# A spilled operand fetched as 32 by 32 blocks and turned by VectorE, in five of eight groups of a four-layer graph network

## The chip, the cores and the metric

The kernel runs on one core of one Trainium2 chip, in one launch. The metric is the device time of the launch in microseconds, the median of several runs. The profile's engine names are used: PE is TensorE, DVE is VectorE, ACT is ScalarE, POOL is GpSimd, SP is SyncE, which here only issues DMAs.

## The reference

The input `x` has 16 batches of 512 nodes with 128 channels; `adj` is a 512 by 512 matrix. Four layers follow one another, and each is added to its input and layer-normalised over the channels:

```python
x = _layernorm(x + _L0_gnn_ref(x, adj, ...), axis=-1)
x = _layernorm(x + _L1_gnn_ref(x, adj, ...), axis=-1)
x = _layernorm(x + _L2_gnn_ref(x, adj, ...), axis=-1)
x = _layernorm(x + _L3_gnn_ref(x, adj, ...), axis=-1)
```

The change concerns the end of the second one. Its batch normalisation needs sums over all batches, so its outputs are first written out and scaled later:

```python
x = agg.reshape(-1, d)
h = jax.nn.relu(_batchnorm(x @ W1.T + b1, g1, be1))
out = h @ W2.T + b2
out = _batchnorm(out, g2, be2)
```

The third layer is two graph convolutions and then LSTM cells over windows of 1, 2, 3 and 4 nodes. The fourth is eight Euler steps with `adj`, computed as powers of a matrix.

## The kernel before

`first_half` computes the first two layers for all batches. It leaves the second layer's outputs, before their batch normalisation, in DRAM as `o2_spill` (printed `o_spill`), one image of 128 channels (partitions) by 512 nodes for each batch, and the first layer's results as `x1_spill`. `second_half` computes the rest in 8 groups of `GB = 2` batches, `g = 0` to 7; `n = 2g + j` counts batches.

A group passes through a pipeline of steps. In step `g` the LSTM cells of group `g` run (eleven of them, `c = 0` to 10: cells 0 and 1 are window length 1, one for each batch; 2 and 3 are length 2; 4 to 6 length 3; 7 to 10 length 4), and between the cells stand pieces of other work: the fourth layer of group `g - 1`, its last part and the output of group `g - 2`, and the front of group `g + 1`. Which piece stands behind which cell is written out by hand in lists, one table for each engine: `FILL_PE`, `FILL_ACT`, `FILL_DVE`, `FILL_POOL`, `FILL_SP`. List 0 stands behind cell 0, list 1 behind cell 1, and so on to list 10, which stands behind the last cell. Steps 2 to 6 use the `FILL` tables and carry the fronts of groups 3 to 7; step 1 uses `NEXT`, step 0 `ONCE`, the start `START`. Every engine works through its own list in order and waits on semaphores.

The front of a batch runs so before the change:

- SP `prep` (L1339, L1342) loads `o2` (printed `xt`) and the first layer's `x2` (printed `x`); for `j = 0` this is `ahead_0` in list 4 of the step before, for `j = 1` `prep_1` in list 0.
- ACT `prep` (L1506) applies the batch normalisation, one ACTIVATE over 128 by 512, with `scale2` and `shift2` as one value per channel, that is per partition. `ahead_0` stands in list 10 of the step before, `prep_1` in list 4.
- PE `turn` (L1908) transposes the four 128 by 128 tiles into a PSUM bank: `turn_0` in list 1, `turn_1` in list 5.
- DVE `turn` adds that bank to `x2` (L1666) and takes the layer normalisation's statistics in four instructions (L1644), in the same lists.
- POOL `turn` (`root`, L1390 to L1399) makes scale and shift of them in ten small instructions.
- ACT `norm` (L1496 four times, L1515) applies them, in list 2 and in list 6; POOL `norm` (L1416) makes the low part, SP `norm` stores the result, and PE `gather0` (list 3 and list 8) multiplies it by `adj`.

Three waits of PE matter around it. Cell 2 begins on PE with

```python
pe.wait_ge(state_ready, CELLS * g + first)
```

with `first = 2`, so it waits for DVE's last instruction of cell 1 (L1638, the low half of the state). A later cell of the same window waits for `st_l` (L1629) before its last four matmuls (L1896). And `power1a_0` (list 2, for the fourth layer) waits for `x3_lo`, which POOL's `x3split_0` (L1425) sets. Products of two split operands are three matmuls, L141 to L143.

Of the kernel before, what the change touches and what calls it, by code (L numbers as in the profile page):

```python
# [54 lines left out]
def program(nc, x_t, adj_n, adj_t, nv1_t, nv2, l0_w, l0_b, w1_t, bn1, w2_t, bn2, wg, bg0, bg1,  # L55
            wih_t, whh_t, bih, bhh, alpha, l3_w_t, l3_d, fc_w, fc_b, eye, out):
    o2_dram = nc.dram_tensor("o2_spill", (B, P, N), F32, kind="Internal").ap()
    x1_dram = nc.dram_tensor("x1_spill", (B, P, N), F32, kind="Internal").ap()
    x2_dram = nc.dram_tensor("x2_spill", (B, P, N), F32, kind="Internal").ap()
    with ExitStack() as whole:  # L60
        def sem(name):
            return whole.enter_context(nc.semaphore(name))
# [29 lines left out]
        second_half(nc, sem, psum, wg_parts, banks, ident, exponent, scale2, shift2, adj_h, adj_l, wih_h, wih_l, whh_h, whh_l,  # L92
                    wg_h, wg_l, gate_bias, row_sums, x1_dram, o2_dram, x2_dram, raw, xt, x1, small, steps, out)

# [877 lines left out]
def second_half(nc, sem, psum, wg_parts, banks, ident, exponent, scale2, shift2, adj_h, adj_l, wih_h, wih_l, whh_h, whh_l,  # L972
# [8 lines left out]
    with ExitStack() as ctx:  # L981
# [215 lines left out]
        def outputs(c, source, ones, twos):  # L1197
# [255 lines left out]
        def _(act):  # L1453
# [45 lines left out]
            def prep(g, j):  # L1499

                n = GB * g + j
                if not at_start(n):
                    act.wait_ge(front_loaded[j], 32 * g)
                elif n == 0:
                    return
                nc.scalar.activation(o2[j], o2[j], ACT.Identity, scale=scale2[:, 0:1], bias=shift2[:, 0:1]).then_inc(normed2, 1)  # L1506
# [361 lines left out]
        def _(pe):  # L1868
# [231 lines left out]
            def bias():  # L2100
                pe.wait_ge(vt_kept, 1)
                pe.wait_ge(bc_kept, 1)
                for t in range(NT):
# [65 lines left out]
```

## Time and profile before

| | us |
|---|---|
| runs of the kernel before, median of 3 | 919.82 (918.21 to 920.14) |
| the profiled execution, its own time | 921.33 |
| its span in the trace | 919.5 |
| one step (steps 2 to 6 repeat within 0.05) | 83.77 |
| PE busy in the span | 885.8 |
| DVE busy | 664.0 |
| ACT busy | 564.0 |
| POOL busy | 339.1 |

The profiled execution lies 1.51 above the median, and 1.8 of it lies outside the span. An instruction's duration includes its latency, and neighbours on one engine overlap by some tenths; what an instruction costs in a stream is the distance from its start to the next one's. The idle time that the profile prints for PE is time between modelled ends, so short waits show only in those distances. The step from 623.20 to 706.97 (step 4) is read as the example of all five.

### The profile page before, as it was taken

How to read it: one execution, taken by the hardware profiler on the slowest of the kernel's cores; microseconds unless marked ns; L12 is line 12 of the kernel's file. 1: busy time of each engine (PE TensorE's matmuls, PEld its weight loads, DVE VectorE, ACT ScalarE, POOL GpSimd, SP SyncE). 2: the span in 40 equal slices, each digit the busy share in tenths (PEclk: the TensorE clock that was granted, in tenths of full speed). 3: DMA queues.
4: the chain of work that ended last, by engine and by line, in shares of the span. 5: the costliest groups of instructions: out<-in, count | busy, mean ns of one | idle time of the engine just before them, and what ended most of it. 6: DMA issues, size and time to landing. Idle time of an engine off the chain costs nothing.

```text
span 919.5 us, 14510 instructions
## 1 busy us (share of the span) xinstructions
PE 885.8 (96%) x4966; PEld 768.8 (84%) x4966; DVE 664.0 (72%) x1583; ACT 564.0 (61%) x1233; POOL 339.1 (37%) x550
## 2 busy tenths in 40 slices
PE   8999999988989999999999999999999999999996
PEld 6888985466877799888989998898989899978986
DVE  5988886886687766667677667767676777665744
ACT  5676766935755674677377547745763775466341
POOL 3777875621023520342153136214421631340221
PEclk9999999999999899999999999999999999999999
DMA  5412201320110101012001201010120001001000
GB/s 188 148 60 71 74 29 69 138 70 1 35 59 1 35 12 47 1 47 65 5 13 35 70 1 36 24 58 1 47 69 1 12 12 47 1 11 36 1 24 23
DMA packets 26594, 38.54 MB, mean 42 GB/s; under 512 B 3333, under 2 KB 12422, under 8 KB 26010
## 3 DMA queue, kind: packets, MB, share of 16 engines
q1 hardware_dynamic: 26088, 36.05, 11.7%
q10 hardware_dynamic: 434, 1.57, 0.5%
q8 instruction: 39, 0.64, 0.3%
q14 instruction: 33, 0.27, 0.1%
HBM read 21.89 MB, written 15.73 MB: 41 GB/s over the span
## 4 chain that ended last, share of the span: by engine, by line
PE 47%; DVE 12%; ACT 8%; POOL 7%; issue 5%; ACTq 0%; DVEq 0%; POOLq 0%
PE psum L141 14%; PE psum L143 13%; PE psum L142 13%; PE psum L1892 2%; PE psum L1893 2%; ACT gate L1465 2%; PE psum L1896 2%; POOL out_rstd L1398 1%; DVE x_stats L1644 1%; DVE x L1666 1%; DVE in_h L1634 1%; POOL node_l L1416 1%; POOL x_rstd L1398 1%; ACT raw L1496 1%; ACT gate L1468 1%
## 5 line engine op out<-in xcount | busy, mean ns | idle before, releaser
L1465 ACT ACTIVATE gate<-psum,gate_bias 128x256 f32<-128x256 f32 (+2 forms) x296 | 143.4, 556 | 62.0 <-PE psum L1896 53.0
L141 PE MATMUL psum<-in_h,wih_h 128*128 128x256 f32 (+2 forms) x312 | 106.8, 342 | 7.3 <-DVE in_l L1638 5.0
L143 PE MATMUL psum<-in_h,wih_l 128*128 128x256 f32 (+2 forms) x312 | 103.5, 332 | 0.0
L142 PE MATMUL psum<-in_l,wih_h 128*128 128x256 f32 (+2 forms) x312 | 102.8, 329 | 0.0
L1432 POOL TENSOR_TENSOR gate<-in_h,in_l 128x512 f32<-128x512 f32 x14 | 17.9, 1307 | 157.5 <-DVE in_l L1638 157.5
L141 PEld LDWEIGHTS psum<-in_h,wih_h 128*128 128x128 f32 x312 | 58.8, 188 | 19.2 <-DVE in_l L1638 9.1
L1468 ACT ACTIVATE gate<-cell 128x512 f32<-128x512 f32 (+2 forms) x80 | 40.3, 503 | 51.2 <-DVE cell L1622 39.7
L1619 DVE TENSOR_TENSOR gate<-gate 128x256 f32<-128x256 f32 (+2 forms) x48 | 24.0, 501 | 61.3 <-ACT gate L1465 61.2
L142 PEld LDWEIGHTS psum<-in_l,wih_h 128*128 128x128 f32 x312 | 59.0, 189 | 5.5 <-issue 0.5
L143 PEld LDWEIGHTS psum<-in_h,wih_l 128*128 128x128 f32 x312 | 58.8, 189 | 4.6
L141 PE MATMUL psum<-e_h,shared 128*128 128x384 f32 x180 | 61.4, 341 | 0.2
L143 PE MATMUL psum<-e_h,shared 128*128 128x384 f32 x180 | 60.6, 336 | 0.0
L142 PE MATMUL psum<-e_l,shared 128*128 128x384 f32 x180 | 60.6, 336 | 0.0
L141 PE MATMUL psum<-shared 128*128 128x512 f32 x140 | 56.9, 407 | 1.3 <-DVE shared L1744 0.7
L1892 PE MATMUL psum<-st_h,whh_h 128*128 128x256 f32 (+2 forms) x192 | 56.7, 313 | 1.2 <-DVE st_h L1627 1.2
L1425 POOL TENSOR_TENSOR shared<-raw,shared 128x512 fp32r<-128x512 f32 x14 | 18.2, 1303 | 104.8 <-ACT shared L1535 104.8
L1893 PE MATMUL psum<-st_h,whh_l 128*128 128x256 f32 (+2 forms) x192 | 56.6, 313 | 0.0
L1390 POOL TENSOR_TENSOR x_mv<-x_stats 128x4 f32<-128x4 f32 x28 | 9.0, 323 | 125.8 <-DVE x_stats L1644 125.8
L143 PE MATMUL psum<-shared 128*128 128x512 f32 x140 | 55.3, 395 | 0.0
L142 PE MATMUL psum<-shared 128*128 128x512 f32 x140 | 55.1, 393 | 0.0
L704 DVE SCALAR_TENSOR_TENSOR mix<-psum,coef,mix 128x256 f32<-128x256 f32 x96 | 46.3, 483 | 9.4 <-ACT mix L508 6.7
L141 PE MATMUL psum<-adj_h,node_h 128*128 128x512 f32 x120 | 47.5, 396 | 2.5 <-POOL node_l L1416 2.5
(403 smaller groups left out, 2887.2 us busy)
## 6 DMA issues: line engine op xcount, KB each, us to landing
x_spill<-x SPq DMA_DIRECT2D x30, 256.0 KB, 2.0
xt<-in_x_t_dram SPq DMA_DIRECT2D x16, 256.0 KB, 2.6
raw<-x_spill SPq DMA_DIRECT2D x16, 256.0 KB, 2.9
o_spill<-xt SPq DMA_DIRECT2D x14, 256.0 KB, 2.0
xt<-o_spill SPq DMA_DIRECT2D x14, 256.0 KB, 3.3
x<-x_spill SPq DMA_DIRECT2D x14, 256.0 KB, 3.5
out_dram<-raw SPq DMA_DIRECT2D x14, 256.0 KB, 2.3
raw<-in_adj_t_dram ACTq DMA_DIRECT2D x1, 1024.0 KB, 9.2
```

Source lines behind the costliest of these rows:

```text
L141: pe.matmul(dst, lh, rh, start=start, stop=False, **kw)
L142: pe.matmul(dst, lh, rl, start=False, stop=False, **kw)
L143: return pe.matmul(dst, ll, rh, start=False, stop=stop, **kw)
L704: chain.link(nc.vector.scalar_tensor_tensor(out=m, in0=scaled_block(t, k), scalar=coef[:, k - 1, t:t + 1], in1=m, op0=ALU.mult, op1=ALU.add))
L1398: chain.link(nc.gpsimd.tensor_tensor(rstd, rstd, exponent[:, 0:rstd.shape[-1]], ALU.pow))
L1425: nc.gpsimd.tensor_tensor(low[:], x3[:, j, :, :], f32(high[:]), ALU.subtract).then_inc(x3_lo, 1)
L1465: nc.scalar.activation(gate[q][:, 0:n], banks[GATE_BANK[q]][:, 0:n], ACT.Tanh if q == 2 else ACT.Sigmoid, bias=gate_bias[:, p - 1, q:q + 1 ...
L1468: nc.scalar.activation(gate[2][:, 0:n], cell[:, 0:n], ACT.Tanh).then_inc(tanh_ready, 1)
L1619: nc.vector.tensor_tensor(gate[0][:, 0:n], gate[0][:, 0:n], gate[2][:, 0:n], ALU.mult)
L1892: pe.matmul(bank, tile(whh_h[:, p - 2, :], q), st_h[:, 0:n], start=False, stop=False)
L1893: pe.matmul(bank, tile(whh_l[:, p - 2, :], q), st_h[:, 0:n], start=False, stop=False)
L1896: pe.matmul(banks[GATE_BANK[q]][:, 0:n], tile(whh_h[:, p - 2, :], q), st_l[:, 0:n], start=False, stop=True).then_inc(gate_sum, 1)
```

## The change

For batches `n >= 6` (groups 3 to 7, ten batches), `prep` on SP fetches `o2` in four DMAs instead of one. Each fills 32 partitions with 16 pieces of 32 nodes (128 bytes) each, so that block (channels a, nodes q) of 32 by 32 lies where its transpose belongs. A channel is now partition `i` of block column `a`, so ACT normalises with four ACTIVATEs of 128 by 4 by 32, each with its own column of a new tile `norm2_blocks`. DVE's `turn` then turns all blocks in place with one STREAM_TRANSPOSE of 128 by 512 and adds; `chain.link` makes the addition wait for it. PE's `turn` is gone for these batches. `gather0` on PE takes over the waits that it had, and SP waits for `x2_summed` where it waited for `o2_turned`.

The lists change too. DVE's and POOL's `turn_0` move from list 1 to list 0, between cell 0 and cell 1; ACT's `prep_1` moves from list 4 to list 2, behind `norm_0`. Once, at the start, DVE copies a selector image of 128 by 512 (`selectors`), PE multiplies it by `norm2` in four matmuls of 2 columns (`block_columns`), and DVE copies the 8 columns out.

```diff
+        norm2 = whole.enter_context(nc.sbuf_tensor("norm2", [P, 2], F32))
+        scale2, shift2 = norm2[:, 0:1], norm2[:, 1:2]
...
+        blocks = 4
+        side = P // blocks
+        norm2_blocks = sb("norm2_blocks", [P, blocks, 2])
...
+        def by_blocks(n):
+            return not isinstance(n, int) or n >= 3 * GB
...
-        FILL_PE = [[], ["giant_2", "giant_3", "giant_0", "giant_1", "turn_0"], ["x3t_0", "power1a_0"],
-                   ["power1b_0", "power2_0", "gather0_0"], ["coefs0_0", "weight0_0"], ["coefs1_0", "turn_1"],
+        FILL_PE = [[], ["giant_2", "giant_3", "giant_0", "giant_1"], ["x3t_0", "power1a_0"],
+                   ["power1b_0", "power2_0", "gather0_0"], ["coefs0_0", "weight0_0"], ["coefs1_0"],
...
-        FILL_ACT = [[], ["x3norm_0", "x3split_0", "evens_h"], ["x3t_0", "norm_0"],
-                    ["power1_0", "power2_0", "evens_l", "out_0", "gather0_0"], ["rest_h", "coefs0_0", "prep_1", "weight0_0", "x3norm_1"],
+        FILL_ACT = [[], ["x3norm_0", "x3split_0", "evens_h"], ["x3t_0", "norm_0", "prep_1"],
+                    ["power1_0", "power2_0", "evens_l", "out_0", "gather0_0"], ["rest_h", "coefs0_0", "weight0_0", "x3norm_1"],
...
-        FILL_DVE = [[], ["ysum_1", "ysum_0", "turn_0"], ["x3t_0", "x3sum_1", "outsum"], ["power1_0", "power2_0", "gather0_0"],
+        FILL_DVE = [["turn_0"], ["ysum_1", "ysum_0"], ["x3t_0", "x3sum_1", "outsum"], ["power1_0", "power2_0", "gather0_0"],
...
-        FILL_POOL = [[], ["x3split_0", "turn_0"], ["norm_0", "outsum", "x3sum_1"], [], [], ["x3split_1", "turn_1"], ["norm_1"], [], [], [],
+        FILL_POOL = [["turn_0"], ["x3split_0"], ["norm_0", "outsum", "x3sum_1"], [], [], ["x3split_1", "turn_1"], ["norm_1"], [], [], [],
...
-                sp.wait_ge(o2_turned, n - 1)
-                sp.dma_start(o2[j], o2_dram[b]).then_inc(front_loaded[j], 16)
+                sp.wait_ge(x2_summed, n - 1)
+                if by_blocks(n):
+                    by_node = o2_dram[b].rearrange("(a i) (t q k) -> q i t a k", a=blocks, q=blocks, k=side)
+                    for q in range(blocks):
+                        rows = o2[j][side * q:side * (q + 1), :].rearrange("i (t a k) -> i t a k", a=blocks, k=side)
+                        sp.dma_start(rows, by_node[q]).then_inc(front_loaded[j], 16)
+                else:
+                    sp.dma_start(o2[j], o2_dram[b]).then_inc(front_loaded[j], 16)
...
+                if by_blocks(n):
+                    act.wait_ge(columns_kept, 1)
+                    for a in range(blocks):
+                        part = o2[j].rearrange("p (t a k) -> p a t k", a=blocks, k=side)[:, a, :, :]
+                        ins = nc.scalar.activation(part, part, ACT.Identity, scale=norm2_blocks[:, a, 0:1], bias=norm2_blocks[:, a, 1:2])
...
+                if by_blocks(n):
+                    dve.wait_ge(normed2, n)
+                    chain.link(nc.vector.transpose(o2[j], o2[j]))
+                    nc.vector.tensor_tensor(flat(x2[j]), o2[j], flat(x2[j]), ALU.add).then_inc(x2_summed, 1)
...
+                    if by_blocks(n):
+                        pe.wait_ge(pre1_ready, GB * g)
+                        need(pe, x3_summed, GB * (g - 1))
+                        need(pe, pre0_ready, n if j == 1 else 0)
```

Three places show how the order of instructions changes. The first is DVE in step 4, from cell 0 to the start of cell 2. A cell of window length 1 is four instructions: the cell, two products of the state, and the low half (`in_l`). `x<-` is the addition of `turn`, BN_STATS on `x` its statistics. Before:

```order
L1617 TENSOR_TENSOR cell<-gate 128x512
L1634 TENSOR_TENSOR in_h<-gate 128x2x256
L1636 TENSOR_TENSOR gate<-gate 128x512
L1638 TENSOR_TENSOR in_l<-gate,in_h 128x2x256
L1617 TENSOR_TENSOR cell<-gate,pre 128x512
L1634 TENSOR_TENSOR in_h<-pre 128x2x256
L1636 TENSOR_TENSOR gate<-pre 128x512
L1638 TENSOR_TENSOR in_l<-gate,in_h 128x2x256
L1738 TENSOR_TENSOR raw<-raw,psum 128x512 x2
L1666 TENSOR_TENSOR x<-psum,x 128x512
L1644 BN_STATS x_stats<-x 128x6 x4
```

The same stretch in the changed kernel:

```order
L1663 TENSOR_TENSOR in_l<-gate,in_h 128x2x256
L1692 STREAM_TRANSPOSE xt<-xt 128x512
L1693 TENSOR_TENSOR x<-xt,x 128x512
L1669 BN_STATS x_stats<-x 128x6 x4
L1642 TENSOR_TENSOR cell<-gate,pre 128x512
L1659 TENSOR_TENSOR in_h<-pre 128x2x256
L1661 TENSOR_TENSOR gate<-pre 128x512
L1663 TENSOR_TENSOR in_l<-gate,in_h 128x2x256
L1768 TENSOR_TENSOR raw<-raw,psum 128x512 x2
```

Six instructions, `turn_0`, now stand ahead of the whole of cell 1, where five stood behind it and behind the two `ysum`.

The second is ACT in the same step, in list 2 (`x3t_0`, `norm_0`) up to the gates and the tanh of cell 3. Before:

```order
L1541 CAST shared<-psum 128x512
L1496 ACTIVATE x<-x,x_shift,x_rstd 128x128 x4
L1515 CAST node_h<-x 128x512
L1465 ACTIVATE gate<-psum,gate_bias 128x512 x4
L1468 ACTIVATE gate<-cell 128x512
```

In the changed kernel:

```order
L1566 CAST shared<-psum 128x512
L1514 ACTIVATE x<-x,x_shift,x_rstd 128x128 x4
L1540 CAST node_h<-x 128x512
L1528 ACTIVATE xt<-xt,norm_blocks 128x4x32 x4
L1483 ACTIVATE gate<-psum,gate_bias 128x512 x4
L1486 ACTIVATE gate<-cell 128x512
```

The four pieces of `prep_1` stand ahead of the gates of cell 3; in list 4 nothing takes their old place.

The third is POOL in the same step: the end of one ten-instruction `root`, and `x3split_0` (`shared<-raw,shared`). Before:

```order
L1397 TENSOR_TENSOR x_rstd<-x_mv 128x4
L1398 TENSOR_TENSOR x_rstd<-x_rstd,exponent 128x4
L1399 TENSOR_TENSOR x_shift<-x_mv,x_rstd 128x4
L1425 TENSOR_TENSOR shared<-raw,shared 128x512
L1390 TENSOR_TENSOR x_mv<-x_stats 128x4
L1391 TENSOR_TENSOR x_mv<-x_stats 128x4
```

In the changed kernel, from the second root's start on:

```order
L1408 TENSOR_TENSOR x_mv<-x_stats 128x4
L1409 TENSOR_TENSOR x_mv<-x_stats 128x4
L1410 TENSOR_TENSOR x_mv<-x_stats 128x4
L1411 TENSOR_SCALAR x_mv<-x_mv 128x4
L1412 TENSOR_SCALAR x_mv<-x_mv 128x4
L1413 TENSOR_SCALAR x_mv<-x_mv 128x4
L1414 TENSOR_TENSOR x_mv<-x_mv 128x4
L1415 TENSOR_TENSOR x_rstd<-x_mv 128x4
L1416 TENSOR_TENSOR x_rstd<-x_rstd,exponent 128x4
L1417 TENSOR_TENSOR x_shift<-x_mv,x_rstd 128x4
L1443 TENSOR_TENSOR shared<-raw,shared 128x512
L1434 TENSOR_TENSOR node_l<-x,node_h 128x512
```

The root of `turn_0` now stands ahead of `x3split_0` instead of behind it.

## Rows read from the trace of the kernel before

**Rows 1.** The page, part 1: busy time of each engine.

```profile
PE 885.8 (96%) x4966; PEld 768.8 (84%) x4966; DVE 664.0 (72%) x1583; ACT 564.0 (61%) x1233; POOL 339.1 (37%) x550
```

**Rows 2.** By stretch: us, busy PE, PEld, DVE, ACT, POOL; PEclk, DMA, GB/s.

```profile
300.00:307.00 7.00, 5.89 (x18) 4.33 (x17) 6.20 (x14) 5.08 (x12) 4.17 (x11) 0.54 0.00 1
...
623.20:706.97 83.77, 83.37 (x500) 75.25 (x499) 60.09 (x133) 53.46 (x120) 28.58 (x56) 1.00 0.10 32
```

**Rows 3.** Timeline of PE, at the lists of cells 1 and 6.

```profile
636.92 0.28 PE L143 MATMUL psum<-shared,pow_l 128*128 128x256 f32 x1
637.04 0.60 PE L1908 MATMUL psum<-ident,xt 128*128 128x128 f32 x4
637.40 0.48 PE L141 MATMUL psum<-in_h,wih_h 128*128 128x512 f32 x1
637.72 0.39 PE L142 MATMUL psum<-in_l,wih_h 128*128 128x512 f32 x1
...
639.93 0.48 PE L141 MATMUL psum<-shared 128*128 128x512 f32 x1
...
669.66 0.32 PE L1893 MATMUL psum<-st_h,whh_l 128*128 128x340 f32 x1
670.11 0.90 PE L1896 MATMUL psum<-st_l,whh_h 128*128 128x340 f32 x4
...
676.61 0.39 PE L143 MATMUL psum<-shared 128*128 128x512 f32 x1
```

**Rows 4.** Timeline of DVE, at cells 0 and 1, and behind cell 5.

```profile
632.49 0.69 DVE L1638 TENSOR_TENSOR in_l<-gate,in_h 128x512 fp32r<-128x512 f32 x1
633.10 0.68 DVE L1617 TENSOR_TENSOR cell<-gate,pre 128x512 f32<-128x512 f32 x1
...
635.82 0.69 DVE L1638 TENSOR_TENSOR in_l<-gate,in_h 128x512 fp32r<-128x512 f32 x1
...
669.98 0.68 DVE L1666 TENSOR_TENSOR x<-psum,x 128x512 f32<-128x512 f32 x1
...
671.48 0.41 DVE L1720 TENSOR_TENSOR raw<-psum,euler_bias 128x256 f32<-128x256 f32 x1
```

**Rows 5.** Instructions of tile xt: one operation's shortest, median and longest ns.

```profile
L849 DVE TENSOR_SCALAR xt<-xt,scale,shift x1: 545/545/545, 186.6 to 186.6; 128x512 f32<-128x512 f32 x1
...
L1506 ACT ACTIVATE xt<-xt,shift,scale x15: 800/817/863, 187.4 to 743.6; 128x512 f32<-128x512 f32 x15
```

**Rows 6.** Groups by line and form: busy us, mean ns, idle before.

```profile
L1496 ACT ACTIVATE x<-x,x_shift,x_rstd 128x128 f32<-128x128 f32 x64 | 26.4, 484 | 22.3 <-POOL x_shift L1399 18.5 <-POOL x_shift L1407 3.8
...
L1425 POOL TENSOR_TENSOR shared<-raw,shared 128x512 fp32r<-128x512 f32 x14 | 18.2, 1303 | 104.8 <-ACT shared L1535 104.8
```

**Rows 7.** Timeline of POOL: first and last of the ten of turn_0.

```profile
639.52 0.20 POOL L1390 TENSOR_TENSOR x_mv<-x_stats 128x4 f32<-128x4 f32 x1 [1.49 <-DVE x_stats L1644]
...
644.19 0.20 POOL L1399 TENSOR_TENSOR x_shift<-x_mv,x_rstd 128x4 f32<-128x4 f32 x1
```

**Rows 8.** Timeline of ACT: ahead_0, what follows it, norm_0, out_0.

```profile
620.36 0.82 ACT L1506 ACTIVATE xt<-xt,shift,scale 128x512 f32<-128x512 f32 x1
623.55 0.62 ACT L1557 CAST shared<-raw 128x512 fp32r<-128x512 f32 x1 [2.37 <-DVE raw L1728]
...
644.42 1.65 ACT L1496 ACTIVATE x<-x,x_shift,x_rstd 128x128 f32<-128x128 f32 x4 [2.79 <-POOL x_shift L1399]
...
653.66 1.65 ACT L1561 ACTIVATE raw<-raw,out_shift,out_rstd 128x128 f32<-128x128 f32 x4 [0.65 <-POOL out_shift L1399]
```

**Rows 9.** Chain of waits of this step, its pieces before cell 7.

```profile
676.32 0.72 DVE in_l L1638 x2
677.08 0.39 PE psum L141
```

**Rows 10.** The page, part 3, and SP's timeline: queue; issue of ahead_0.

```profile
q1 hardware_dynamic: 26088, 36.05, 11.7%
...
572.07 0.50 SPq L1339 DMA_DIRECT2D xt<-o_spill  x1
```

More of the change, by code:

```diff
@@ L91, in program @@
                    wg_h, wg_l, gate_bias, row_sums, x1_dram, o2_dram, raw, xt, x1, small, small_in, steps)
[L92 removed]
+        second_half(nc, sem, psum, wg_parts, banks, ident, exponent, norm2, adj_h, adj_l, wih_h, wih_l, whh_h, whh_l,
                     wg_h, wg_l, gate_bias, row_sums, x1_dram, o2_dram, x2_dram, raw, xt, x1, small, steps, out)
@@ L969, with second_half @@
 ROWS = 2 * BABY
-def second_half(nc, sem, psum, wg_parts, banks, ident, exponent, scale2, shift2, adj_h, adj_l, wih_h, wih_l, whh_h, whh_l,
+def second_half(nc, sem, psum, wg_parts, banks, ident, exponent, norm2, adj_h, adj_l, wih_h, wih_l, whh_h, whh_l,
                 wg_h, wg_l, gate_bias, row_sums, x1_dram, o2_dram, x2_dram, raw, o2_pair, x1_pair, small, steps, out):
@@ L1094, in gathers, with loads @@
             return gat_h[:], gat_l[:]
+        def by_blocks(n):
+            return not isinstance(n, int) or n >= 3 * GB
+        def loads(g):
+            return 32 * min(g, 2) + 16 * (blocks + 1) * max(g - 2, 0)
         def conv_of(n, conv):
             return GB * conv + n + 1 if at_start(n) else 2 * n + conv + 1
+        columns_kept = sem("columns_kept")
         lws_ready, bcols_zero, vpad_zero, weff_done, k_chain = (
@@ L1253, in second_half @@
         TAIL_SP = [["out_0", "out_1"], ["outhalf_1", "outhalf_0"]]
-        START_PE = ["turn_0", "turn_1", "weff", "first_0", "first_1", "gather0_0", "gather0_1", "weight0_0", "weight0_1", "first_2",
+        START_PE = ["turn_0", "turn_1", "weff", "first_0", "first_1", "block_columns", "gather0_0", "gather0_1", "weight0_0", "weight0_1", "first_2",
                     "gather1_0", "gather1_1", "weight1_0", "weight1_1"]
@@ L1258, in second_half @@
                      "first_2", "gather1_0", "gather1_1", "input_0", "input_1"]
-        START_DVE = ["columns", "turn_0", "turn_1", "weff", "conv_bias", "first_0", "row_sum", "first_1", "gather0_0", "gather0_1", "weight0_0", "weight0_1",
+        START_DVE = ["columns", "turn_0", "turn_1", "weff", "conv_bias", "selectors", "first_0", "row_sum", "first_1", "block_columns", "gather0_0", "gather0_1", "weight0_0", "weight0_1",
                      "first_2", "bcols", "gather1_0", "gather1_1", "weight1_0", "input_0", "weight1_1", "input_1"]
@@ L1278, in second_half @@
                    ["weight0_0", "coefs0_0"], ["coefs1_0", "turn_1"]] + FILL_PE[6:]
-        NEXT_ACT = [[], ["lift"] + FILL_ACT[1], FILL_ACT[2] + ["split_e"], ["power1_0", "power2_0", "evens_l", "gather0_0"],
+        NEXT_ACT = [[], ["lift"] + FILL_ACT[1], ["x3t_0", "norm_0", "split_e"], ["power1_0", "power2_0", "evens_l", "gather0_0"],
                     ["rest_h", "prep_1", "weight0_0", "coefs0_0", "x3norm_1"],
@@ L1283, in second_half @@
                     ["power1_0", "power2_0", "gather0_0"], ["weight0_0", "coefs0_0"], ["coefs1_0", "turn_1"]] + FILL_DVE[6:]
-        NEXT_POOL = FILL_POOL[:2] + [["norm_0", "split_e", "x3sum_1"]] + FILL_POOL[3:]
+        NEXT_POOL = [[], ["x3split_0", "turn_0"], ["norm_0", "split_e", "x3sum_1"]] + FILL_POOL[3:]
         def step(g, cell_step, pieces, fill, lstm=True, l3=True, front=True, done=True):
@@ L1501, in prep @@
                 n = GB * g + j
+                if n == 0:
+                    return
                 if not at_start(n):
[L1503 to L1506, printed above, removed]
+                    act.wait_ge(front_loaded[j], loads(g))
+                if by_blocks(n):
[3 more added lines that the diff above has]
+                        ins = nc.scalar.activation(part, part, ACT.Identity, scale=norm2_blocks[:, a, 0:1], bias=norm2_blocks[:, a, 1:2])
+                else:
+                    ins = nc.scalar.activation(o2[j], o2[j], ACT.Identity, scale=norm2[:, 0:1], bias=norm2[:, 1:2])
+                ins.then_inc(normed2, 1)
             def norm(g, j):
@@ L1664, in turn @@
                 n = GB * g + j
-                dve.wait_ge(o2_turned, n + 1)
-                nc.vector.tensor_tensor(flat(x2[j]), FB[j][:], flat(x2[j]), ALU.add).then_inc(x2_summed, 1)
+                if by_blocks(n):
+                    dve.wait_ge(normed2, n)
+                    chain.link(nc.vector.transpose(o2[j], o2[j]))
+                    nc.vector.tensor_tensor(flat(x2[j]), o2[j], flat(x2[j]), ALU.add).then_inc(x2_summed, 1)
+                else:
+                    dve.wait_ge(o2_turned, n + 1)
+                    nc.vector.tensor_tensor(flat(x2[j]), FB[j][:], flat(x2[j]), ALU.add).then_inc(x2_summed, 1)
                 dve.wait_ge(x2_summed, n + 1)
@@ L1809, in weff, with selectors, block_columns @@
                                                op0=ALU.mult, op1=ALU.add).then_inc(b_kept, 1)
+            def selectors():
+                nc.vector.tensor_copy(bp[:, 5:5 + blocks, :].rearrange("p a (q i) -> p a q i", q=blocks),
+                                      ident[:].rearrange("p (a i) -> p a i", a=blocks).unsqueeze(2).broadcast_to([P, blocks, blocks, side])
+                                      ).then_inc(lws_ready, 1)
+            def block_columns():
+                dve.wait_ge(weff_done, 2)
+                nc.vector.tensor_copy(norm2_blocks[:].rearrange("p a s -> p (a s)"), banks[0][:, P:P + 2 * blocks]).then_inc(columns_kept, 1)
             def spread_bias():
@@ L2043, in weff, with block_columns @@
                 pe.matmul(tile(banks[0][:], 0), lws[:], lw[:], start=True, stop=True).then_inc(weff_done, 1)
+            def block_columns():
+                pe.wait_ge(lws_ready, 2)
+                for a in range(blocks):
+                    mm = pe.matmul(banks[0][:, P + 2 * a:P + 2 * (a + 1)], bp[:, 5 + a, :], norm2[:], start=True, stop=True)
+                mm.then_inc(weff_done, 1)
             def product(k, t):
@@ L2113, in _ @@
                             "inner": inner, "giant": giant, "hturn": hturn,
-                            "weff": weff, "first": lambda t: product(0, t), "second": lambda t: product(1, t),
+                            "weff": weff, "block_columns": block_columns, "first": lambda t: product(0, t), "second": lambda t: product(1, t),
                             "square": square, "cube": cube, "fourth": fourth, "fc": fc, "offset": offset, "lift": lift, "bias": bias},
```

4 lines of the change are left out of this document (1 added, 3 removed).

## The prediction

> **What bounds the kernel now.** I read the busy times first [rows 1]: PE is busy 885.8 of 919.5 us, every other engine has a quarter or more of the span free. Then one step by stretch [rows 2]: in the 83.77 us from 623.20 PE is busy 83.37 at a granted clock of 1.00, the 2.4 GHz level. So in steps 2 to 6, the only ones that the change touches, every microsecond taken from PE is a gain and every wait of PE a loss, unless a wait that already exists swallows it. Then PE's own timeline, start to start [rows 3]. The reader is to see two things there. The four transposes of `turn_0` begin at 637.04, cell 2's first matmul at 637.40, and its second 0.32 later where neighbours stand 0.23 apart: the turn costs PE 0.36 + 0.09 = 0.45 us. And at 670.11 the last matmuls of cell 6 (its 128x340 neighbours are 0.155 apart) start 0.29 late: PE waits there for DVE's `st_l`. Last comes DVE's timeline against PE's [rows 4]: cell 1's last instruction starts at 635.82, lasts 0.69 and ends at 636.51. PE would reach cell 2 at 637.04 if the turn were gone. That is 0.53 us of room, and no more.
>
> **Term 1, PE's turns.** Ten turns of 0.45 us leave PE, two in each of five steps: 4.5 us if PE stays fed.
>
> **Term 2, `turn_0` ahead of cell 1 on DVE.** Behind cell 0's `in_l`, DVE now runs the transpose, the addition and the statistics, and only then cell 1. The addition and statistics take 1.50 us of DVE's time: from 669.98 to the next instruction at 671.48 [rows 4]; that the addend is read from SBUF and no longer from PSUM I cost at nothing (DVE's products and additions of this size, `cell<-gate,pre` here, take 0.68 either way). The transpose has no row. From below it is bounded by the shortest one-source pass over 128x512, 0.545 us [rows 5], plus the 0.03 that a linked successor starts later: 0.57. From above I take every block read twice, 2 x 0.68 = 1.36 [rows 4]. I take 0.70, nearest to the linked 128x512 instructions of DVE, since it is one pass over the same elements with a link behind it. By the Trainium skill, page VectorE: DVE Perf Modes, section The three transpose paths, VectorE turns 128x128 in bf16 in 311 ns; four of them would be 1.24 us, an estimate, and the sum of terms 2 to 4 would rise by 0.54 in two places of a step, 5.4 us in all.
>
> So cell 1 starts on DVE 0.70 + 1.50 = 2.20 us later. Nothing absorbs that: from 633.10 DVE goes through cell 1 with no wait but the tanh's own latency, and ACT, which had idled before that tanh, only follows. `in_l` ends at 636.51 + 2.20 = 638.71. PE reaches cell 2 at 637.04 and waits until 638.76 (0.05 for the handover, as between the two pieces of [rows 9]: 676.32 + 0.72 = 677.04, PE at 677.08). Against 637.40 before, cell 2 starts **1.36 us later**, the saved turn already counted. Queued behind DVE's turn are also the two `ysum`, some 0.7 us each, which PE's `x3t_0` needs; that stands behind all of cell 2's matmuls, so they are in time.
>
> **Term 3, POOL's order.** The root of `turn_0` now stands ahead of `x3split_0`. DVE's statistics end at 633.10 + 0.70 + 1.58 = 635.38; the root took 644.39 - 639.52 = 4.87 us [rows 7], so it ends near 640.3, and `x3split_0`, 1.30 us [rows 6], near 641.6. PE's `power1a_0` starts 639.93 - 637.40 = 2.53 us after cell 2 [rows 3], now at 641.3. Another 0.3 us of wait; 0 to 0.6, since the root's small instructions stretch with what DVE does beside them.
>
> **Term 4, list 5.** Here PE loses nothing by the turn but cannot keep the 0.45: at cell 6 it already waits for `st_l`. What shortens that chain is the earlier root. ACT's `norm_0` waited 2.79 us for POOL, and `out_0` 0.65 us [rows 8], because POOL came to the output's root only behind `norm_0`'s low part; both waits go, so `out_0` and, in order behind it, the gates of cell 4, `rest_h`, the casts and the gates of cell 5 come 0.65 us sooner, and `st_l` with them. PE would arrive 0.45 sooner and had waited 0.29, so it takes nearly all of it. But behind `st_l` DVE now does `turn_1` with its transpose, 0.70 us more ahead of cell 6, and cell 7 on PE waits for cell 6's `in_l` with no room [rows 9]. Net -0.65 + 0.70 = **+0.05 us** at cell 7.
>
> **What costs nothing.** ACT's normalisation grows from 0.82 us [rows 5] to four pieces at the pace of `norm_0`, 1.65 [rows 8]. `ahead_0` has 2.37 us of idle time behind it [rows 8]. `prep_1` comes into list 2, where the 2.79 us wait has gone, and with 1.65 us it fits; without that cover cell 3's gates, and PE behind them, would be late by up to 1.65. The block loads: 4 DMAs of 512 pieces each. A packet of the hardware queue took 0.117 x 16 x 919.5 / 26088 = 0.066 us of one DMA engine [rows 10], so 2048 of them take about 8.4 us on 16 engines, and `ahead_0`'s load is issued at 572.07 and used at 620.36, 48.3 us later [rows 8, 10]. SP issues three more DMAs at 0.50 us, with nothing urgent behind them. The one-off work at the start, some 1 us of DVE and PE, lies beside waits of PE for POOL there and I count it as 0.
>
> **Sum.** 1.36 + 0.30 + 0.05 = 1.71 us a step, times 5 = 8.6 us on the profiled execution's 921.33, giving 929.9. The median of the runs lies 1.5 lower: **928.4**. With both terms at their low ends (transpose 0.57, no wait for POOL) it is 1.23 + 0 - 0.08 = 1.15 a step, 925.6; at the high ends (1.36, 0.6) 2.02 + 0.6 + 0.71 = 3.33 a step, 936.5.
>
> **Rivals.**
>
> *Half of the loss is won back later.* PE might keep in list 5 all it can: its 0.45 and the waits at cells 6 and 7, 0.29 and 677.08 - 676.61 - 0.23 = 0.24 us [rows 3], 0.98 in all, if `turn_1` hides in DVE's free time. Against it: between `st_l` and cell 6 DVE has none. With the short transpose that is 1.23 - 0.98 = 0.25 a step, 921.1, no change that a measurement can tell (0.2%, 1.8 us, is about its limit). Chance 0.07.
>
> *The other side: DVE's turn finds cover and PE keeps its 4.5 us.* Mechanism: cell 1 on DVE isn't what cell 2 on PE waits for, or DVE gets to it in time. The point from which it decides is 0.53 us of added work ahead of cell 1 for no wait at all, and 0.53 + 0.45 = 0.98 for no loss; the addition and statistics alone are 1.50. For it speaks that ACT's waits for POOL's roots [rows 8] are relieved by this order. Price: 919.82 - 4.5 = 915.3. Chance 0.08.
>
> *The block loads come late.* A load that takes 60 us instead of 8 would hold ACT, and all behind it, for 12 us in each of ten batches: 120 us, near 1040. The rows of the queue speak against it by a factor of seven. The Trainium skill (VectorE: DVE Perf Modes, The three transpose paths) warns that a plain DMA that does the transpose by strides is 19 times slower than the crossbar's; here runs of 128 bytes stay whole, and no run here shows such a transfer. Chance 0.04.
>
> *PE's waits cost it the clock.* Once, from 300 to 307, the granted clock was 0.54 in the mean, mostly the 1.2 GHz level [rows 2], in step 1, whose PE list has more waits than the later ones; that cost 0.46 x 7 = 3.2 us. A fall in each of five steps would add 16: 944. Against it, the waits of 1.7 us are short beside a step in which PE is otherwise never idle. Chance 0.05.
>
> **Numbers.** The forecast keeps 0.76, with its own range of 925.0 to 934.5 (the high end of the transpose is unlikely). The range for 8 in 10 reaches down to the first rival: 921.0 to 934.5. Slower by over 0.2%: 0.76 + 0.04 + 0.05 = 0.85; within: 0.07; faster: 0.08.
>
> **What would show it.** In step 4's counterpart PE's cell 2 waits 1.5 to 1.9 us for `in_l` of cell 1, a wait that the profile names; DVE's cell 1 follows its statistics without a gap; STREAM_TRANSPOSE takes 0.55 to 0.75 us; ACT waits for POOL neither before `norm_0` nor before `out_0`; the period of steps 2 to 6 is 85.5 us instead of 83.77; steps 0, 1 and 7 keep their lengths. A period under 83.8 would prove term 2 wrong; one over 87 would mean the transpose or the loads.

## The result and the profile after

The changed kernel takes **927.76 us**, the median of 4 runs (926.56 to 929.04), against 919.98 us for the kernel before, 4 runs in the same job (918.21 to 920.80). The ratio is 1.0089, with a 95% interval of 1.0074 to 1.0104: slower by 6.8 to 9.6 us. The forecast was 928.4.

The profiled execution took 927.98 us, 6.65 more than that of before. Its span, cut at the start of `hturn` in list 10, the cut of [rows 2], divides so:

| stretch | before | after | difference |
|---|---|---|---|
| start to step 2 | 372.16 | 370.13 | -2.0 |
| steps 2 to 6, each | 83.62 to 83.77 | 85.12 to 85.19 | +7.2 in all |
| step 7 | 74.67 | 76.23 | +1.6 |
| from there to the end | 54.1 | 54.1 | 0 |

Only the second line is the change's own. The first varies from one execution to the next: over the nine profiled kernels of this document it lies between 368.56 and 372.98, and `plain_loads` below, which differs from the changed kernel up to there in one batch's load and normalisation alone, reached step 2 at 372.07. The third is a fall of the clock, read further down. So the change costs 1.37 to 1.50 us in each of five steps. (The five steps of the kernel before are alike within 0.15, not within 0.05 as the table of before says.)

A word on names: the step from 623.20, called step 4 above and in the expectations, is the fourth of the five that repeat; counted from step 2 it is step 5. All five are alike, so no number hangs on it.

The page of the changed kernel, part 1, answers to [rows 1], and the queue of part 3 to [rows 10]:

```profile
PE 883.4 (95%) x4934; PEld 766.2 (83%) x4934; DVE 670.9 (72%) x1595; ACT 571.9 (62%) x1263; POOL 339.0 (37%) x550
...
q1 hardware_dynamic: 45768, 36.06, 12.9%
```

PE is busy 2.4 us less, DVE 6.9 more, and the queue moves the same bytes in 19680 more packets.

The same kernel by stretch (us, busy PE, PEld, DVE, ACT, POOL; PEclk, DMA, GB/s): the counterpart of the step of [rows 2], step 7, and two pieces of step 7.

```profile
625.56:710.75 85.19, 82.66 (x492) 74.46 (x491) 61.35 (x135) 54.99 (x126) 27.62 (x56) 1.00 0.12 32
795.89:872.12 76.23, 72.12 (x447) 66.65 (x445) 48.53 (x112) 44.65 (x102) 18.00 (x34) 0.98 0.05 15
823.00:826.00 3.00, 0.90 (x4) 0.45 (x3) 2.96 (x6) 2.64 (x8) 2.81 (x7) 1.00 0.00 0
826.50:830.00 3.50, 3.50 (x14) 3.50 (x14) 1.93 (x5) 3.19 (x8) 1.61 (x3) 0.52 0.27 75
```

In the step PE is busy 82.66 of 85.19 us, where it was 83.37 of 83.77: 0.7 us of work is gone, and 2.5 us lie idle where 0.4 did. Where, the timeline of PE in the changed kernel shows, around cell 2, cell 6 and cell 7 (columns as in [rows 3]; the bracket is idle time and what ended it):

```profile
639.32 0.28 PE L143 MATMUL psum<-shared,pow_l 128*128 128x256 f32 x1
641.23 0.50 PE L141 MATMUL psum<-in_h,wih_h 128*128 128x512 f32 x1 [1.64 <-DVE in_l L1663]
...
643.93 0.50 PE L141 MATMUL psum<-shared 128*128 128x512 f32 x1
...
673.22 0.32 PE L1932 MATMUL psum<-st_h,whh_l 128*128 128x340 f32 x1
673.37 0.81 PE L1935 MATMUL psum<-st_l,whh_h 128*128 128x340 f32 x4
...
679.79 0.39 PE L143 MATMUL psum<-shared 128*128 128x512 f32 x1
680.88 0.39 PE L141 MATMUL psum<-in_h,wih_h 128*128 128x256 f32 x1 [0.70 <-DVE in_l L1663]
```

Cell 2 begins 1.91 us after the matmul before it, where 0.12 is its pace: **1.79 us** of waiting, and the trace names the low part of cell 1 on DVE. The wait for `st_l` inside cell 6 is gone (0.15 from 673.22 to 673.37). Cell 7 waits 1.09 - 0.23 = 0.86, where it waited 0.24.

DVE in the changed kernel, the counterpart of [rows 4]:

```profile
634.92 0.69 DVE L1663 TENSOR_TENSOR in_l<-gate,in_h 128x512 fp32r<-128x512 f32 x1
635.53 0.70 DVE L1692 STREAM_TRANSPOSE xt<-xt 128x512 f32<-128x512 f32 x1
636.27 0.69 DVE L1693 TENSOR_TENSOR x<-xt,x 128x512 f32<-128x512 f32 x1
637.00 0.87 DVE L1669 BATCH_NORM_STATS2 x_stats<-x 128x6 f32<-128x128 f32 x4
637.79 0.67 DVE L1642 TENSOR_TENSOR cell<-gate,pre 128x512 f32<-128x512 f32 x1
...
640.49 0.69 DVE L1663 TENSOR_TENSOR in_l<-gate,in_h 128x512 fp32r<-128x512 f32 x1
```

There is no gap from 635.53 to 637.79: transpose 0.74 from start to start, addition and statistics 1.52. Cell 1's last instruction ends at 641.18, and PE starts at 641.23.

POOL and ACT in the changed kernel: the first and the last instruction of `turn_0`'s root and `x3split_0` ([rows 7]), then ACT in list 2 and `out_0` ([rows 8]).

```profile
637.95 0.57 POOL L1408 TENSOR_TENSOR x_mv<-x_stats 128x4 f32<-128x4 f32 x1 [2.28 <-DVE x_stats L1669]
...
642.43 0.20 POOL L1417 TENSOR_TENSOR x_shift<-x_mv,x_rstd 128x4 f32<-128x4 f32 x1
642.58 1.30 POOL L1443 TENSOR_TENSOR shared<-raw,shared 128x512 fp32r<-128x512 f32 x1
```

```profile
645.46 1.65 ACT L1514 ACTIVATE x<-x,x_shift,x_rstd 128x128 f32<-128x128 f32 x4
647.14 0.62 ACT L1540 CAST node_h<-x 128x512 fp32r<-128x512 f32 x1
647.67 1.65 ACT L1528 ACTIVATE xt<-xt,norm_blocks 128x128 f32<-128x128 f32 x4
650.57 1.84 ACT L1483 ACTIVATE gate<-psum,gate_bias 128x512 f32<-128x512 f32 x3 [1.25 <-PE psum L1935]
...
656.51 0.51 ACT L1495 CAST in_l<-in_l 128x170 fp32r<-128x170 f32 x1
656.83 1.67 ACT L1586 ACTIVATE raw<-raw,out_shift,out_rstd 128x128 f32<-128x128 f32 x4
```

`x3split_0` ends at 643.88 and PE's `power1a_0` starts at 643.93, so POOL does hold PE there (read from these positions; no run moves POOL's root alone). ACT waits for POOL neither before `norm_0` (2.79 before) nor before `out_0` (0.65 before), and behind `prep_1` it still waits 1.25 us for PE: the four pieces cost nothing in this place.

### The profile page after: what moved, and what is told of

The parts are those of the page before. It is cut to its first block, busy times and chain, and to the rows that moved or that the text cites. A ratio compares the mean times of both kernels' runs of the same rounds, so it can differ in the third digit from the quotient of the medians.

```text
span 926.2 us, 14533 instructions
## 1 busy us (share of the span) xinstructions
PE 883.4 (95%) x4934; PEld 766.2 (83%) x4934; DVE 670.9 (72%) x1595; ACT 571.9 (62%) x1263; POOL 339.0 (37%) x550
## 4 chain that ended last, share of the span: by engine, by line
PE 50%; DVE 16%; ACT 8%; issue 3%; POOL 1%; ACTq 0%; DVEq 0%; POOLq 0%
PE psum L141 14%; PE psum L142 13%; PE psum L143 13%; PE psum L1932 2%; PE psum L1931 2%; PE psum L1935 2%; ACT gate L1483 2%; DVE in_h L1659 2%; ACT gate L1486 1%; DVE in_l L1663 1%; DVE cell L1642 1%; DVE gate L1661 1%; DVE x_stats L1669 1%; DVE st_l L1654 1%; ACT raw L1586 1%
## 5 line engine op out<-in xcount | busy, mean ns | idle before, releaser
L1408 POOL TENSOR_TENSOR x_mv<-x_stats 128x4 f32<-128x4 f32 x28 | 11.3, 404 | 132.1 <-DVE x_stats L1669 132.1
```

## The experiments

My theory: the step is longer by DVE's work ahead of cell 1, by a little of POOL's behind it, and by the transpose in list 5, which eats what the earlier root brings. Rivals: the block loads or the four ACTIVATEs cost the time; it is the order of the lists and not the transpose; PE's turns were worth 4.5 us, which something still hides. The kernel before had 919.96 in the job of the first four (18 runs) and 919.48 in that of the last three (23 runs). "Period" is the length of the same step as above, from one profiled execution.

**`no_flip0`**: the change, without the transpose of the even batches.

```diff
-                    chain.link(nc.vector.transpose(o2[j], o2[j]))
+                    if j == 1:
+                        chain.link(nc.vector.transpose(o2[j], o2[j]))
```

> The changed kernel without the STREAM_TRANSPOSE of the even batches (turn_0); its blocks stay unturned, so that part of the result is left out. Theory (DVE's work ahead of cell 1 is what PE waits for): cell 1 starts 0.74 us sooner, the transpose and its link, and PE's wait before cell 2 falls from 1.79 us to about 1.05; the period of a step goes from 85.19 to about 84.45 us, five times that is 3.7 us, so 924.1. Rival (the loss comes from the block loads, ACT's four pieces or the slower clock): no change, 927.8. In both, PE's wait before cell 7 stays at 0.86.

Measured: 923.02 (920.39 to 925.84, 7 runs), ratio 1.0043 (1.0026 to 1.0059); period 84.45 instead of 85.19, **0.74 less**. PE at cell 2 in this kernel:

```profile
635.60 0.27 PE L143 MATMUL psum<-shared,pow_l 128*128 128x256 f32 x1
636.71 0.50 PE L141 MATMUL psum<-in_h,wih_h 128*128 128x512 f32 x1 [0.84 <-DVE in_l L1663]
```

The wait falls from 1.79 to 1.11 - 0.12 = 0.99. The whole of this transpose, 0.74 from start to start, lies on the path.

**`no_flips`**: the change, with neither transpose.

> The changed kernel with neither STREAM_TRANSPOSE; the blocks of all ten batches stay unturned. Theory (term 4: the transpose of turn_1 stands ahead of cell 6 on DVE and cell 7 on PE waits for it, without room): besides the 3.7 us of turn_0, PE's wait before cell 7 falls from 0.86 to about 0.12, period about 83.7, time 920.4. Rival (list 5 has room, its transpose is hidden): the same as without the transpose of turn_0 alone, 924.1.

Measured: 920.29 (918.66 to 922.28, 12 runs), ratio 1.0008 (0.9996 to 1.0019); period 83.78. PE before cell 7 in this kernel:

```profile
675.99 0.39 PE L143 MATMUL psum<-shared 128*128 128x512 f32 x1
676.44 0.39 PE L141 MATMUL psum<-in_h,wih_h 128*128 128x256 f32 x1
```

The second transpose costs 84.45 - 83.78 = 0.67 a step, nearly its whole length, and cell 7's wait is back to 0.22. Together the two make 1.41 of the 1.42 us a step. **Without its transposes the change is worth nothing, in either direction**: it has taken 0.9 us of turns off PE in every step, and the period is 83.78 where it was 83.77.

**`plain_loads`**: the change, with `o2` fetched in one DMA and normalised by one ACTIVATE (transposes kept).

```diff
-                if by_blocks(n):
-                    by_node = ...
...
+                sp.dma_start(o2[j], o2_dram[b]).then_inc(front_loaded[j], 16)
...
-                    for a in range(blocks):
...
+                    ins = nc.scalar.activation(o2[j], o2[j], ACT.Identity, scale=norm2_blocks[:, 0, 0:1], bias=norm2_blocks[:, 0, 1:2])
```

> The changed kernel with o2 loaded by one DMA of whole rows for every batch, and normalised in one ACTIVATE with the first block's columns; everything else is kept, so the result of ten batches is not the layer's. Theory (loads and pieces are hidden): no change, 927.8 within 0.7. Rival (30 more DMAs, 15360 more packets and 1.1 us more ACT work for each batch cost something): 1 to 4 us faster.

Measured: 927.99 (925.37 to 928.85, 6 runs), ratio 1.0085 (1.0069 to 1.0102); period 85.20. That is the changed kernel's time: loads and pieces cost nothing. In the changed kernel the block loads (L1355) and the whole ones that are left (L1357) read so, by source line on SP:

```profile
L1355 SPq DMA_DIRECT2D xt<-o_spill x40: 568/637/1208, 306.4 to 690.1; - x40
...
DMA to landing us min/median/max: 2.3/2.6/3.7
```

```profile
L1357 SPq DMA_DIRECT2D xt<-o_spill x4: 425/430/431, 195.3 to 267.0; - x4
...
DMA to landing us min/median/max: 2.7/3.2/3.8
```

A quarter load in runs of 128 bytes lands 2.6 us after its issue (the longest 3.7), where the estimate was 8.4 for four and the room 48.3. The Trainium skill (VectorE: DVE Perf Modes, The three transpose paths) warns of a copy that transposes by strides, 19 times slower when the innermost destination stride is large. These loads keep runs of 32 nodes whole, so they are not that case, and no run here tests it.

**`turn0_list1`**: the change, with the lists of before: `turn_0` in list 1 on DVE and POOL, `prep_1` in list 4 on ACT.

```diff
-        FILL_DVE = [["turn_0"], ["ysum_1", "ysum_0"], ...
+        FILL_DVE = [[], ["ysum_1", "ysum_0", "turn_0"], ...
-        FILL_POOL = [["turn_0"], ["x3split_0"], ...
+        FILL_POOL = [[], ["x3split_0", "turn_0"], ...
```

> The changed kernel with turn_0 of DVE and POOL back in list 1 behind the ysum, and prep_1 of ACT back in list 4. Theory: PE no longer waits before cell 2 (-1.79 us a step), but the chain turn_0, root, norm_0, output root, out_0, gates, st_l, turn_1, cell 7 gets both transposes, 0.74 us each, on top of the 0.29 and 0.24 us by which PE waited for it in the kernel before, so cells 6 and 7 wait: period 83.77 + 1.4 = 85.2, time 927. The move to list 0 then gains nothing and loses nothing. Rival (turn_0 ahead of cell 1 is the whole loss, and moving it back frees PE's 0.9 us a step): period 82.9 to 83.8, time 915 to 920.

Measured: 926.40 (925.46 to 928.11, 6 runs), ratio 1.0077 (1.0063 to 1.0091); period 84.91. PE inside cell 6 in this kernel:

```profile
674.20 0.32 PE L1932 MATMUL psum<-st_h,whh_l 128*128 128x340 f32 x1
675.05 0.58 PE L1935 MATMUL psum<-st_l,whh_h 128*128 128x340 f32 x2 [0.54 <-DVE st_l L1654]
```

Cell 2 no longer waits at all; the time comes back as 0.62 before cell 4, 0.85 - 0.16 = 0.69 inside cell 6 and 0.88 before cell 7. The wait before cell 4 (for DVE's `in_l`) was not in my theory. The old order with the transposes is only 0.28 us a step better than the new one. Two edits went back together here, `turn_0` and `prep_1`, and I didn't part them.

**`before_list0`**: the kernel before, with `turn_0` moved to list 0 on PE, DVE and POOL (the tables of steps 2 to 6 alone). Nothing of blocks or transposes.

```diff
-        FILL_PE = [[], ["giant_2", "giant_3", "giant_0", "giant_1", "turn_0"], ...
+        FILL_PE = [["turn_0"], ["giant_2", "giant_3", "giant_0", "giant_1"], ...
-        FILL_DVE = [[], ["ysum_1", "ysum_0", "turn_0"], ...
+        FILL_DVE = [["turn_0"], ["ysum_1", "ysum_0"], ...
-        FILL_POOL = [[], ["x3split_0", "turn_0"], ...
+        FILL_POOL = [["turn_0"], ["x3split_0"], ...
```

> The kernel before with nothing but turn_0 moved from list 1 to list 0 on PE, DVE and POOL, in steps 2 to 6; transposes stay on PE. Theory: 1.50 us of DVE work stand ahead of cell 1, in_l of cell 1 ends at 636.51 + 1.50 = 638.01, cell 2 starts 0.66 us later than before; but POOL's root comes sooner, out_0 no longer waits 0.65 us, and PE's waits of 0.29 and 0.24 us at cells 6 and 7 go: net +0.13 a step, 920.6. Rival (a late cell 2 is not won back anywhere): +0.66 a step, 923.3.

Measured: 921.57 (919.03 to 924.17, 12 runs), ratio 1.0017 (1.0000 to 1.0034); period 83.87, 0.10 more. PE at cell 2 in this kernel:

```profile
634.35 0.28 PE L143 MATMUL psum<-shared,pow_l 128*128 128x256 f32 x1
635.44 0.50 PE L141 MATMUL psum<-in_h,wih_h 128*128 128x512 f32 x1 [0.82 <-DVE in_l L1638]
```

Cell 2 starts 0.66 later in the step than before, by the prediction's own sum: 1.50 of DVE's work, less 0.53 of room, less the 0.36 that PE's turn no longer stands there, plus 0.05 for the handover. But the waits at cells 6 and 7 are gone, and 0.56 of the 0.66 is back by the step's end. And it stands beside `no_flips`, which has the same order of `turn_0` on DVE and POOL without PE's turns: 83.87 against 83.78. They differ in the block loads and in `prep_1`'s pieces and place too, but those are hidden in this order, as `plain_loads` and ACT's wait of 1.25 us show. **The 0.9 us of turns that left PE were worth 0.09 us a step.** Both have somewhere to hide in this order. In the kernel before PE pauses ahead of cell 1 for ACT's gates, and in `before_list0` `turn_0` stands just in that pause. The kernel before, then `before_list0`:

```profile
629.28 0.47 PE L141 MATMUL psum<-in_h,wih_h 128*128 128x512 f32 x1 [0.15 <-ACT gate L1465]
```

```profile
626.35 0.60 PE L1908 MATMUL psum<-ident,xt 128*128 128x128 f32 x4
626.70 0.48 PE L141 MATMUL psum<-in_h,wih_h 128*128 128x512 f32 x1
```

Cell 1 starts 629.28 - 623.20 = 6.08 into the step in the first and 626.70 - 620.58 = 6.12 in the second. And of the 0.45 us that `turn_1` frees in `no_flips`, 0.22 goes into the wait before cell 7, which `before_list0` doesn't have, and about 0.1 more into cell 7's second matmul, which then comes 0.23 behind the first and not 0.12.

**`early_turn0`**: the change, with all of `turn_0` on DVE and POOL a step sooner, in list 10 of the step before, where PE has a long stretch of work; `ahead_0` on ACT moves from list 10 to the head of list 9.

```diff
-        FILL_DVE = [["turn_0"], ["ysum_1", "ysum_0"], ...
-                    ["coefs1_1", "gather1_1", ...
+        FILL_DVE = [[], ["ysum_1", "ysum_0"], ...
+                    ["coefs1_1", "turnahead_0", "gather1_1", ...
-        FILL_POOL = [["turn_0"], ["x3split_0"], ...
-                     ["whole", "x3first"]]
+        FILL_POOL = [[], ["x3split_0"], ...
+                     ["whole", "turnahead_0", "x3first"]]
...
-        AHEAD_NAMES = ("ahead",)
+        AHEAD_NAMES = ("ahead", "turnahead")
```

> The changed kernel with the whole turn_0 (transpose, addition, statistics, and POOL's root) one step earlier, in list 10, where DVE waits 2.23 us for ACT's gat_h; ahead_0 of ACT moves to the head of list 9 for it. Theory: PE's wait before cell 2 (1.79 us) goes, the one before cell 7 (0.86) stays, period 85.19 - 1.8 - 0.14 = 83.25, time 927.8 - 5 x 1.94 = 918.1. Rival (DVE is simply too full, wherever the turn stands something waits for it): 921 or more.

Measured: 918.13 (915.57 to 920.70, 12 runs), ratio 0.9967 (0.9949 to 0.9984); period 83.17. DVE in list 10 of this kernel, and PE before cell 7:

```profile
616.52 0.70 DVE L1692 STREAM_TRANSPOSE xt<-xt 128x512 f32<-128x512 f32 x1
617.25 1.47 DVE L1693 TENSOR_TENSOR x<-xt,x 128x512 f32<-128x512 f32 x1
618.76 0.88 DVE L1669 BATCH_NORM_STATS2 x_stats<-x 128x6 f32<-128x128 f32 x4
```

```profile
673.76 0.39 PE L143 MATMUL psum<-shared 128*128 128x512 f32 x1
674.85 0.39 PE L141 MATMUL psum<-in_h,wih_h 128*128 128x256 f32 x1 [0.70 <-DVE in_l L1663]
```

The same instructions, 3 us of them on DVE, no longer stand ahead of anything that PE waits for: 2.02 us a step less than the changed kernel, and 0.60 less than before. Of PE's waits for the turns only cell 7's 0.86 is left.

**`early_flips`**: `early_turn0`, and the transpose of `turn_1` by itself in list 3 (its data lie ready since `prep_1` in list 2); its addition and statistics stay in list 5.

```diff
+            def flip(g, j):
+                dve.wait_ge(normed2, GB * g + j)
+                chain.link(nc.vector.transpose(o2[j], o2[j]))
...
-                    ... ["power1_0", "power2_0", "gather0_0"],
+                    ... ["power1_0", "power2_0", "flip_1", "gather0_0"],
```

> As the run before, and the transpose of turn_1 alone also sooner, in list 3 ahead of gather0_0, where DVE waits 0.36 to 1.06 us for ACT. Theory: PE's wait before cell 7 falls from 0.86 to about 0.15, period 82.5, time 914.5, faster than both kernels. Rival (the transpose delays gather0_0's low part and by it weight0_0 and cell 5): 918.

Measured: **913.79** (911.97 to 915.93, 6 runs), ratio 0.9923 (0.9900 to 0.9946); period 82.52. The transpose on DVE in list 3 of this kernel, PE before cell 7, and the step by stretch:

```profile
646.16 1.28 DVE L1744 TENSOR_TENSOR shared<-psum,shared 128x512 fp32r<-128x512 f32 x2
647.36 0.70 DVE L1690 STREAM_TRANSPOSE xt<-xt 128x512 f32<-128x512 f32 x1
648.09 0.69 DVE L1709 TENSOR_TENSOR gat_l<-psum,gat_h 128x512 fp32r<-128x512 f32 x1
```

```profile
668.60 0.39 PE L143 MATMUL psum<-shared 128*128 128x512 f32 x1
669.06 0.39 PE L141 MATMUL psum<-in_h,wih_h 128*128 128x256 f32 x1
```

```profile
616.41:698.93 82.52, 82.26 (x493) 74.38 (x492) 61.97 (x135) 55.07 (x126) 27.80 (x57) 1.00 0.13 33
```

Cell 7's wait falls from 0.86 to 0.23, and the period by 0.65. PE is idle 0.26 us in the step. The 1.25 us against the kernel before are more than the 0.9 of turns, because the wait inside cell 6 (0.29, and 0.09 behind it: from `st_l`'s matmuls to the next one PE takes 670.85 - 670.11 = 0.74 in the kernel before and 0.65 here) is gone as well, while the one before cell 7 is as long as before. This kernel does exactly what the change does. By the medians it takes 5.7 us less than the kernel before, by the ratio 7.1 (5.0 to 9.2); the period gives 5 x 1.25 = 6.3. It beats both kernels.

## Why the prediction was right, and where its terms were off

The sum was 1.71 us a step and the step shows 1.42. Positions are from the step's start, 623.20 before and 625.56 after.

**Term 1**, 0.90 a step, held nearly as a size: a step has 0.71 us less of PE's busy time, which is the two 0.36; the two 0.09 are a delay of the next matmul and no busy time. It held as a warning too, since it was to count only if PE stays fed: between `no_flips` and `before_list0` it is worth 0.09.

**Term 2**, cell 2 later by 1.36: it is 14.20 before and 15.67 after, **1.47**. The transpose was taken as 0.70 from start to start and is 0.74; the addition and the statistics 1.50 and are 1.52; DVE's cell 0 itself comes 0.07 later (its last instruction starts at 9.29 and 9.36). The rest of the chain held within 0.02, and PE starts 0.05 after DVE's last instruction ends, as forecast. The Trainium skill's 311 ns for 128x128 in bf16 (VectorE: DVE Perf Modes, The three transpose paths), taken four times, was an estimate of 1.24; the trace has 0.70 for 128x512 in fp32, so the nearest rows of this kernel were the better guide.

**Term 3**, POOL's order, 0.30: `power1a_0` stands at 16.73 before and 18.37 after, so 1.64 - 1.47 = **0.17** came here. The root took 642.63 - 637.95 = 4.68 instead of 4.87, and its start had slid with term 2.

**Term 4**, list 5, +0.05: cell 7 stands at 53.88 before and 55.32 after, 1.44 later where `power1a_0` was 1.64 later, thus **-0.20**. This is the mis-sized term, by 0.25. Its parts were right in kind: the earlier root brings `out_0` and all behind it forward, and cell 7 waits for cell 6's `in_l`, which the transpose delays. The largest error is the 0.65 for `out_0`. It is the idle time that the profile prints, and not a distance from start to start. ACT's last cast ahead of `out_0` ([rows 8]) in the kernel before:

```profile
652.51 0.50 ACT L1477 CAST in_l<-in_l 128x170 fp32r<-128x170 f32 x1
```

`out_0` starts 653.66 - 652.51 = 1.15 behind it, and in the changed kernel 656.83 - 656.51 = 0.32, so 0.83 us was won there. DVE's `st_l` starts at 45.27 before and 46.10 after, 0.83 later where `power1a_0` is 1.64 later: it comes **0.81** sooner relative to that point, not 0.65. From `turn_1`'s first instruction on DVE to the one behind its statistics it is 2.25, where it was 1.50: 0.75 more, where 0.70 was charged. And from cell 6's `in_h` on DVE (51.36 and 52.94) to cell 7 on PE the changed kernel needs 0.14 less, because `in_h` and `in_l` are a little shorter; why, no run shows. Together -0.81 + 0.75 - 0.14 = -0.20.

**What was to cost nothing** did cost nothing: ACT's pieces and the loads by `plain_loads`, `prep_1` by the 1.25 us that ACT still waits behind it. Steps 0, 1 and 7 show no cost of the change; step 7's 1.6 us in the profiled execution are the clock's, and the one-off work at the start would be lost in the spread of 4 us up to step 2.

**The numbers.** 5 x 1.42 = 7.1 us, against 7.8 between the medians, whose interval begins at 6.8; forecast were 8.6. The three terms were off by +0.11, -0.13 and -0.25 a step, 1.5 us too much in all. That the forecast of 928.4 lies only 0.6 from the median is in part luck: the runs of the changed kernel came out 0.7 us above what its steps account for.

**The rivals.** *Half won back*: no, though the earlier root's gain is real, as `before_list0` shows (0.56 a step). In the change PE comes to cell 7 only 0.82 later than before, half of the 1.64, but waits there for DVE, where the second transpose stands. *DVE finds cover*: not where the change puts it; 2.26 us of DVE's work came ahead of cell 1, against a point of decision at 0.98. `early_turn0` and `early_flips` show that cover exists elsewhere in the step. *Loads late*: excluded. *The clock*: in steps 2 to 6 the granted clock stays at 1.00 behind waits of 1.79 us; excluded for this wait. Step 7's fall is another matter, below.

## What to carry to other kernels

Where one engine is busy without a break and the others have a quarter of their time free, that free time is not free everywhere: ask of each piece moved onto such an engine what stands behind it in that engine's order, and by how much that next piece is ahead of the busy engine (here 0.53 us at cell 1, against 2.26 of new work). Taking work off the busy engine pays only if the work doesn't end in front of a wait: 0.9 us of matmuls gone, 0.09 won, until DVE's part was put into list 10 and list 3, which brought 1.25 us a step over the kernel before. Moving a piece costs one table entry, so try its place before judging the piece. And price every wait from start to start, on the helper engines too: the idle time printed for `out_0` was 0.65, and its going brought 0.83.

## What the runs showed of the hardware

**An instruction with two SBUF inputs takes two to three times as long beside POOL.** In `early_turn0` the addition `x<-xt,x`, both inputs in SBUF, takes 1.47 us, against 0.69 in the changed kernel. POOL in the same kernel, which runs beside it:

```profile
615.62 2.56 POOL L1450 TENSOR_TENSOR gate<-in_h,in_l 128x512 f32<-128x512 f32 x2 [21.16 <-DVE in_l L1663]
```

The transpose before it, with one input, keeps its 0.70 beside the same instructions. All five additions of list 10 take 1.47 or 1.48 there, and the five of list 5, which have no POOL instruction beside them, 0.69. The changed kernel shows it too, with a subtraction: beside POOL's `x3split_1` the 128x340 `st_l` takes 1.58 where its neighbours take 0.51.

```profile
671.58 1.30 POOL L1443 TENSOR_TENSOR shared<-raw,shared 128x512 fp32r<-128x512 f32 x1 [12.39 <-ACT shared L1560]
```

```profile
671.12 0.51 DVE L1653 TENSOR_TENSOR gate<-gate 128x340 f32<-128x340 f32 x1
671.66 1.58 DVE L1654 TENSOR_TENSOR st_l<-gate,st_h 128x340 fp32r<-128x340 f32 x1
```

The Trainium skill (SBUF — State Buffer, Who interferes with whom) says that a Vector instruction with two SBUF inputs contends with a GpSimd one that reads SBUF; the traces agree, with 0.8 to 1.1 us for one such meeting. DVE's instruction ends 0.54 us after POOL's in the first case and 0.36 in the second, so it looks as if it did its work only once POOL's was done. No experiment here moves POOL's instruction away, so the cause is read from the overlap and not shown by a run. `st_l` takes 1.58 or 1.59 in each of the steps 2 to 6 of the kernel before as well, and cells 6 and 7 of PE wait behind it; whether another place for `x3split_1` would win that microsecond wasn't tried.

**The clock falls in one execution and not in the next.** Step 7 of the changed kernel has PE idle for 2.10 us up to 825.74, and from 826.50 to 830.00 the granted clock is 0.52 in the mean, about the 1.2 GHz level. The kernel before has the same wait, 2.11 us, and no such fall; nor has any of the seven experiments, with 74.66 to 74.72 us for the step against 76.23. In step 1 the fall that [rows 2] shows comes in every profiled execution, but lasts 3.4 us in four and 6.8 in five, whichever the edit. The fall in step 7 cost 1.6 us (76.23 - 74.67), and step 1 takes 80.87 and 81.05 us with the short fall (`no_flip0`, `before_list0`), 82.50 and 82.53 with the long one (`no_flips`, `turn0_list1`). Falls go along with the spread of the runs: of the 23 runs of the kernel before in the second job, the eight with the lowest mean granted clock (0.991 to 0.993) took 920.95 to 924.16 us, the other fifteen (0.995 and 0.996) 917.95 to 921.56. A difference of 2 us between two single profiles thus says nothing of the edit, while the period of the steps, which repeats within 0.2 us inside a profile, does.
